# A graph and expert layer on one core: twelve gather tiles moved from the indirect DMA to SP, and reciprocal roots worked out by VectorE

## The reference

```python
# x [6250, 256]; 106250 edges (src, dst), sorted by dst; all float32
def gnn(X, src, dst, W_root, W_neigh, b):          # row = src, col = dst
    deg = segment_sum(1, row);  denom = max(deg, 1)
    neigh = segment_sum(X[col], row) / denom
    H = relu(X @ W_root + neigh @ W_neigh + b)
    gg = segment_sum((H[row] - H[col]) ** 2, row) / denom
    return tanh(gg)
def ffn(f, ...):                                   # 6 experts, the best 2 of them
    p = softmax(relu(f @ rw1 + rb1) @ rw2 + rb2)
    w = softmax(top2(p))
    return sum over the 2 of w * (relu(relu(f @ W1 + b1) @ W2 + b2) @ W3 + b3)
x = x + gnn(layernorm(x), ...)
x = x + ffn(layernorm(x), ...)                     # layernorm = (x - m) / sqrt(v + 1e-5)
```

## Time and profile before

| | |
|---|---|
| median of 3 runs | 3124.15 us (3121.96 to 3128.59) |
| the profiled execution | 3120.48 us, span 3118.7 us |
| PE | 2496.6 us busy (80%) |
| POOL | 2136.4 us busy (69%) |
| DVE | 1986.1 us busy (64%) |
| ACT | 935.7 us busy (30%) |
| mean granted clock of PE | 0.840 of full speed |
| DMA | 329.43 MB, 106 GB/s |
| edges sorted, nodes normalised | 0 to 327 us |
| first pass | 327 to 1428 us |
| H | 1428 to 1496 us |
| second pass | 1496 to 2608 us |
| first four groups, first sort | 2608 to 2678 us |
| experts, with the other groups beside them | 2678 to 3119 us |

### The profile page before, as it was taken

How to read it: one execution, slowest core, us unless ns; L and a number is a source line. 1 busy time by engine, 2 the same in 40 slices (tenths; PEclk the granted TensorE clock), 3 DMA queues, 4 the chain that set the end, 5 groups by cost and what they waited for, 6 DMA issues and landing times.

```text
span 3118.7 us, 37405 instructions
## 1 busy us (share of the span) xinstructions
PE 2496.6 (80%) x8562; PEld 1286.7 (41%) x8562; DVE 1986.1 (64%) x5179; ACT 935.7 (30%) x2562; POOL 2136.4 (69%) x2203
## 2 busy tenths in 40 slices
PE   5564688887888787889788888888888887898995
PEld 3454344343444444346322222222222222687995
DVE  8999555555554554545676767677777767566664
ACT  3689000000000000003333333333333334565653
POOL 4377677777777777778777777777777773224566
PEclk7555677777777877768999999999999998999998
DMA  0212433333333333332533333333333334344445
GB/s 29 83 4 39 136 105 106 106 105 105 106 105 105 106 105 105 106 105 92 175 105 112 105 104 104 105 105 105 105 104 105 105 105 128 100 125 130 150 146 150
DMA packets 172728, 329.43 MB, mean 106 GB/s; under 512 B 43611, under 2 KB 108833, under 8 KB 172519
## 3 DMA queue, kind: packets, MB, share of 16 engines
q0 software_dynamic: 103872, 259.13, 29.5%
q1 hardware_dynamic: 68647, 67.92, 6.6%
HBM read 284.40 MB, written 42.11 MB: 105 GB/s over the span
## 4 chain that ended last, share of the span: by engine, by line
PE 30%; POOL 26%; DMA 17%; issue 14%; DVE 10%; ACT 2%; DVEq 1%; SPq 0%; POOLq 0%; ACTq 0%
POOL arena L1047 25%; PE ps L1082 13%; DMA arena<-xn_table,graph 11%; PE ps L1905 7%; DMA arena<-h_table,graph 5%; PE ps L1879 3%; DVE big L1118 2%; DVE big L855 2%; PE ps L1208 2%; PE ps L1137 1%; DVE arena L847 1%; PE ps L1857 1%; DVE node L787 1%; PE ps L1139 1%; DVE arena L851 1%
## 5 line engine op out<-in xcount | busy, mean ns | idle before, releaser
L1082 PE MATMUL ps<-arena,graph 128*128 128x258 f32 (+1 forms) x3512 | 1714.0, 594 | 392.2 <-DMA arena<-xn_table,graph 158.9
L1118 DVE TENSOR_TENSOR big<-ps,big 128x258 f32 (+1 forms) x1756 | 982.0, 559 | 574.8 <-PE ps L1082 564.2
L1082 PEld LDWEIGHTS ps<-arena,graph 128*128 128x128 f32 x3512 | 640.1, 219 | 1450.8 <-DMA arena<-h_table,graph 747.0
L1047 POOL DMA_INDIRECT arena<-h_table,graph x878 | 840.4, 957 | 270.3 <-issue 233.2
L1047 POOL DMA_INDIRECT arena<-xn_table,graph x878 | 830.8, 946 | 282.6 <-issue 161.5
L1111 DVE TENSOR_SCALAR graph<-iota,graph 128x128 f32<-128x128 f32 x1756 | 517.5, 295 | 303.9 <-PE ps L1082 258.3
L1063 ACT ACTIVATE arena<-arena 128x256 f32<-128x256 f32 x878 | 362.6, 416 | 746.7 <-DMA arena<-h_table,graph 736.9
L1146 ACT ACTIVATE late<-ps 128x256 f32<-128x256 f32 x49 | 18.8, 383 | 924.0 <-PE ps L1127 924.0
L1485 POOL DMA_INDIRECT arena<-xn_table,node x118 | 121.5, 1030 | 240.4 <-PE ps L1857 122.9
L594 PE MATMUL ps<-big,arena 128*128 128x128 f16 x832 | 98.2, 307 | 85.2 <-ACT big L631 85.2
L541 POOL DMA_INDIRECT edge_list<-big x64 | 113.4, 1772 | 67.0 <-issue 49.4
(11 more groups left out here) (293 smaller groups left out, 1872.3 us busy)
## 6 DMA issues: line engine op xcount, KB each, us to landing
y_table<-big SPq DMA_DIRECT2D x57, 256.0 KB, 2.4
arena<-xn_table,graph POOLq DMA_INDIRECT x878, 2.7
arena<-h_table,graph POOLq DMA_INDIRECT x878, 2.7
xn_table<-node SPq DMA_DIRECT2D x7, 896.0 KB, 5.1
h_table<-node SPq DMA_DIRECT2D x7, 896.0 KB, 4.1
node<-in_x SPq DMA_DIRECT2D x1, 6144.0 KB
late<-h_table SPq DMA_DIRECT2D x12, 512.0 KB, 5.7
big<-in_x SPq DMA_DIRECT2D x12, 512.0 KB, 4.6
```

Source lines behind the costliest of these rows:

```text
L1047: e.indirect_dma_start(out=row, out_offset=None, in_=table, in_offset=bass.IndirectOffsetOnAxis(ap=idx[:, k:k + 1], axis=0)).then_inc(s_ro ...
L1082: e.matmul(out_, hot[:, k % HOTS, :], moving, start=True, stop=True).then_inc(s_sum[i], 1)
L1118: e.tensor_tensor(block, ps[a % BANKS][:, 0:width], block, ALU.add).then_inc(s_add[i], 1)
```

## The change

Six tiles of the 878 in either pass (tiles 145, 291, 437, 583, 729 and 875) are no longer gathered by POOL. SP fetches them: it loads the 128 row numbers of a tile into registers, 16 per load, and issues one DMA of 1 KB for each row. To that end DVE copies the six columns of row numbers to `sp_cols`, SP writes them to DRAM and reads two tiles' numbers at a time into one partition (`sp_row`). SP's tiles have two slots of their own, and POOL's ring has 16 slots in both passes. In the second pass SP issues five of its tiles ahead of the wait for the biases' products, and the sixth behind it.

The roots by ACT (`act_norm_root`, L1828) are gone. `dve_rsqrt` makes the reciprocal root from the variance alone: a first guess by a shift and a multiply-add on the integer form, then a step of four and a step of three operations, nine in all where it was five, each waiting for the one before. The statistics called `early` are no longer pulled ahead. In the plan route step 1 stands in the tick of step 0, and all that follows in a route moves one tick forward.

```diff
+    RING = 16
+    SPT = 6
+    LISTS = 2
@@ the first span, in dve_edges
                 if k == SUMS_AT + 2 * NA + 4:
-                    e.wait_ge(s_root, 1)
+                    e.wait_ge(s_var, 1)
                     dve_rsqrt(e, 0, NA)
@@ def act_nodes(e)
-                if b == 2 * CH - 1:
-                    act_norm_root(e, 1)
-                if b == NA + CH - 1:
-                    act_norm_root(e, 2)
@@ def dve_rsqrt(e, b0, n)
-            var, root, quot = (nsc[:, i, b0:b0 + n] for i in range(3))
-            e.reciprocal(quot, root).then_inc(s_v, 1)
...
-            e.reciprocal(rstd[:, b0:b0 + n], root).then_inc(s_v, 1)
+            var, guess, part = (nsc[:, i, b0:b0 + n] for i in range(3))
+            e.tensor_scalar(guess.bitcast(I32), var.bitcast(I32), 1, None, ALU.logical_shift_right).then_inc(s_v, 1)
+            e.wait_ge(s_v, v.up())
+            e.tensor_scalar(guess.bitcast(I32), guess.bitcast(I32), -1.0, float(0x5f3759df), ALU.mult,
+                            ALU.add).then_inc(s_v, 1)
+            for shift_by, factor in ((5.0, 1.0), (0.5625, -0.5 * 0.375 ** 3)):
+                e.wait_ge(s_v, v.up())
+                e.tensor_tensor(part, guess, guess, ALU.mult).then_inc(s_v, 1)
+                e.wait_ge(s_v, v.up())
+                e.scalar_tensor_tensor(part, part, factor, var, ALU.mult, ALU.mult).then_inc(s_v, 1)
+                if factor == 1.0:
+                    e.wait_ge(s_v, v.up())
+                    e.scalar_tensor_tensor(part, part, -10.0 / 3.0, part, ALU.add, ALU.mult).then_inc(s_v, 1)
+                e.wait_ge(s_v, v.up())
+                out_ = guess if factor == 1.0 else rstd[:, b0:b0 + n]
+                e.scalar_tensor_tensor(out_, part, shift_by, guess, ALU.add, ALU.mult).then_inc(s_v, 1)
             e.wait_ge(s_v, v.up())
@@ def dve_nodes(e)
-            dve_stats(e, a1, early)
             dve_scale(e, 1)
-            dve_stats(e, early, a2)
+            dve_stats(e, a1, a2)
...
             e.wait_ge(s_idx, 1)
+            step = NT // SPT
+            e.tensor_copy(sp_cols[:, :], idx[:, step - 1:SPT * step:step]).then_inc(s_cols, 1)
+        BY_SP = [(j + 1) * (NT // SPT) - 1 for j in range(SPT)]
+        BY_POOL_K = [k for k in range(NT) if k not in BY_SP]
+        def slot_of(k):
+
+            return RING + BY_SP.index(k) % 2 if k in BY_SP else BY_POOL_K.index(k) % RING
+
+        def sp_pass(e, i, tiles):
+
+            for j in tiles:
+                k = BY_SP[j]
+                if j >= 2:
+                    e.wait_ge(s_sum[i], BY_SP[j - 2] + 1)
+                if j % LISTS == 0:
+                    e.dma_start(sp_row, sp_list[j:j + LISTS, :].rearrange("(a j) p -> a (j p)", a=1).bitcast(I32)
+                                ).then_inc(s_sprow, 16)
+                    e.wait_ge(s_sprow, 16 * (2 + (i * SPT + j) // LISTS))
+                slot = slot_of(k)
+                row = rows2[:, slot, :] if i else rows1[:, slot, 0:D]
+                for p0 in range(0, P, 2 * OFFS):
+                    _, at_ = nc.values_load_multi_w_load_instructions(
+                        sp_row[0:1, j % LISTS * P + p0:j % LISTS * P + p0 + 2 * OFFS], engines=[mybir.EngineType.SP], min_val=0,
+                        max_val=NB * P - 1, skip_runtime_bounds_check_because="an edge's source is below N")
+                    for p, place in enumerate(at_, p0):
+                        e.dma_start(row[p:p + 1, :], (h_table if i else xn_table)[bass.ds(place, 1), :]
+                                    ).then_inc(landed(k, i)[0], 16)
+
+        def sp_first_pass(e):
+            e.wait_ge(s_cols, 1)
+            e.dma_start(sp_list.rearrange("j p -> p j"), sp_cols[:, :], allow_slow_non_contiguous=True).then_inc(s_sprow, 16)
+            e.wait_ge(s_sprow, 16)
+            e.wait_ge(s_xnout, 16 * NCH)
+            e.wait_ge(s_one, 1)
+            sp_pass(e, 0, range(SPT))
@@ def pool_pass(e, i)
-            for k in range(NT):
-                slot = k % ring
-                if k >= ring:
-                    e.wait_ge(s_sum[i], k - ring + 1)
+            for n, k in enumerate(BY_POOL_K):
+                slot = slot_of(k)
+                if n >= RING:
+                    e.wait_ge(s_sum[i], BY_POOL_K[n - RING] + 1)
@@ def route_of(pair, t)
                 put(t, "route", pair[0], 0)
-                put(t + 1, "route", pair[0], 1)
+                put(t, "route", pair[0], 1)
                 for j, g in enumerate(pair):
                     for h in half_of(g):
-                        put(t + 1 + j, "norm", g, h)
-                        put(t + 2 + j, "flip", g, h)
+                        put(t + j, "norm", g, h)
+                        put(t + 1 + j, "flip", g, h)
                     for step in (3, 4, 5):
-                        put(t + step + j, "route", g, step)
-                return t + 5 + len(pair)
+                        put(t + step - 1 + j, "route", g, step)
+                return t + 4 + len(pair)
@@ def route_slowly(pair, t)
                 put(t, "route", pair[0], 0)
-                put(t + 1, "route", pair[0], 1)
-                t += 2
+                put(t, "route", pair[0], 1)
+                t += 1
@@ def sp_records(e)
+            sp_pass(e, 1, range(SPT - 1))
             e.wait_ge(s_b3, 1 + NE)
             for g in range(1, HR):
                 sp_h_again(e, g)
+            sp_pass(e, 1, range(SPT - 1, SPT))
@@ def act_route(e, g, step)
-            if step == 0 and g in span_of:
-                b0, m = span_of[g]
-                e.wait_ge(s_ag, span_no[g] + 1)
-                e.activation(nsc[:, 1, b0:b0 + m], nsc[:, 0, b0:b0 + m], ACT.Sqrt).then_inc(s_sq2, 1)
```

More of the change, by code:

```diff
@@ L155, in gnn_moe_kernel @@
         local = graph[:, HOTS * P + NT:HOTS * P + NT + NTR]
+        sp_cols = sb("sp_cols", [P, SPT], U32)
+        sp_row = arena[0:1, SLOTS * W1 + 2 * D - LISTS * P:SLOTS * W1 + 2 * D].bitcast(I32)
+        assert SLOTS * D <= SLOTS * W1 + 2 * D - LISTS * P and (RING + 2) * W1 <= SLOTS * D
         offs = graph[0:1, HOTS * P + NT + NTR:HOTS * P + NT + NTR + P * TJ].bitcast(I32)
@@ L367, in gnn_moe_kernel @@
         s_one = sem("ones_set")
-        s_row = [sem(f"row_in_{i}") for i in range(SLOTS)]
+        s_row = [sem(f"row_in_{i}") for i in range(RING)]
+        s_rowsp = [sem(f"row_by_sp_in_{i}") for i in range(6)]
+        s_cols = sem("sp_rows_picked")
+        s_sprow = sem("sp_rows_moved")
         s_hot = [sem(f"edge_hot_made_{i}") for i in (1, 2)]
@@ L1024, in beside @@
             return k // STRIDE if k % STRIDE == 0 and k // STRIDE <= NB else None
-        def rows_in(k, i):
-            if i == 0:
-                return 16 * (k // SLOTS + 1)
-            ring = SLOTS - SQUARES
-            return 16 * (len(range(k % ring, NT, SLOTS)) + k // ring + 1)
+        BY_SP = [(j + 1) * (NT // SPT) - 1 for j in range(SPT)]
+        BY_POOL_K = [k for k in range(NT) if k not in BY_SP]
+        assert SPT % 2 == SPT % LISTS == 0 and RING + 2 + SQUARES <= SLOTS
+        def slot_of(k):
+            return RING + BY_SP.index(k) % 2 if k in BY_SP else BY_POOL_K.index(k) % RING
@@ new lines, in landed @@
+        def landed(k, i):
+            if k in BY_SP:
+                n = i * SPT + BY_SP.index(k)
+                return s_rowsp[n % len(s_rowsp)], 16 * P * (n // len(s_rowsp) + 1)
+            n, slot = BY_POOL_K.index(k), slot_of(k)
+            return s_row[slot], 16 * (i * len(range(slot, len(BY_POOL_K), RING)) + n // RING + 1)
+        def sp_pass(e, i, tiles):
[16 more added lines that the diff above has]
+                                    ).then_inc(landed(k, i)[0], 16)
@@ L1033, in pool_pass @@
+        def sp_first_pass(e):
[5 more added lines that the diff above has]
+            sp_pass(e, 0, range(SPT))
         def pool_pass(e, i):
-            table, ring = ((xn_table, SLOTS), (h_table, SLOTS - SQUARES))[i]
+            table = (xn_table, h_table)[i]
             if i == 0:
@@ L1057, in act_pass @@
                 if i:
-                    ring = SLOTS - SQUARES
-                    slot, sq = k % ring, ring + k % SQUARES
-                    e.wait_ge(s_row[slot], rows_in(k, 1))
+                    slot, sq = slot_of(k), RING + 2 + k % SQUARES
+                    e.wait_ge(*landed(k, 1))
                     if k >= SQUARES:
@@ L1318, in side_work @@
                 for j, g in enumerate(pair):
-                    put(at + 6 + j, "best", g)
+                    put(at + 5 + j, "best", g)
             x1_of(pairs[1][0], t)
@@ L1327, in side_work @@
                     y = route_slowly(pair, t)
-                    t += 2 + len(pair)
+                    t += 1 + len(pair)
                 t = y
@@ L1824, in act_route @@
             n = len(blocks)
[L1825 to L1829 removed]
+            if step == 3:
                 e.wait_ge(s_rh, g + 1)
@@ L1964, in _ @@
             sp_nodes(e)
+            sp_first_pass(e)
             sp_h(e)
```

27 lines of the change are left out of this document (6 added, 21 removed).

## The result

| | before | after |
|---|---|---|
| median | 3124.16 us (3119.66 to 3128.63, 20 runs) | 3115.27 us (3110.54 to 3122.48, 20 runs) |
| ratio | | 0.9974, 95% interval 0.9967 to 0.998 |
| profiled execution | 3120.48 us, span 3118.7 | 3113.14 us, span 3111.4 |
| granted clock | 0.840 | 0.843 |

The change makes the kernel 0.26% faster, 9 us. The forecast was 23 us, with 3113 as the upper end of its range. The direction was right, and the size was outside.

A forecast was written before the change was run, and what follows sets the result against it. POOL's gathers were taken to bound both passes, PE the expert stage. The terms +1.8 - 15.1 - 4 - 6 = -23.3 us took 3124.15 to 3101 us, range 3090 to 3113.

The forecast's parts named there:

- The bound in the passes: Both passes: each lasts as long as POOL's 878 gathers, and a gather taken off saves its period, 1.251 or 1.262 us.
- The gathers, -15.1 us: Both passes: twelve gathers leave POOL, saving 7.5 us in the first and 7.6 us in the second; smaller ring costs nothing.
- What SP pays: SP in the passes: 0.6 us per row, 77 us per tile, upper bound 0.99, hidden behind POOL's gathers.
- Rival A: Passes: SP is too slow, from 1.29 us per row, and sets their length; about 3305 us, chance 0.12.
- The fixed 2.0 us: SP's row DMAs: paid one after another, 256 us per tile against 183 allowed; the prediction went by the trace instead.
- The estimate for the DMA engines: Both passes: 16 packets per row, 24,600 more packets, 74 us of the engines' time, share 0.36 becoming 0.39.
- The start, +1.8 us: Before the first gather: DVE's four extra operations per root call delay it by 1.8 us, between 0 and 3.
- The lead stage, -4 us: Between second pass and experts: earlier variance, a table load gone and ticks saved gain 4 us, range 1.5 to 6.
- Beside the experts, -6 us: Expert stage: fewer ACT table loads shrink PE's gaps, less DVE's longer piece; 6 us won, range 0 to 11.
- four gaps of PE: Expert stage, 2680 to 2920: gaps of 1.4, 2.35, 2.49 and 3.6 us, near 10 together, laid to ACT's table loads and root waits.
- B: Whole kernel: gathers bring 15 us, roots nothing, as DVE's longer piece costs PE what ACT's tables did; 3111 us, chance 0.18.

The follow-up runs named there:

- after_again: The changed kernel, run again unaltered for a second trace: 3112.29 us, ratio 0.9972 to the kernel before.
- before_again: The kernel before, run again unaltered for a second trace: 3120.94 us, ratio 0.9995.
- list_twice: The changed kernel with SP's list of row numbers written twice, to two places, behind xn_table's writes: 3110.26 us, ratio 0.9968 to the kernel before.
- gathers_only: The kernel before plus only SP's part of the change, roots by ACT and plan as before: 3488.62 us on a chip where before takes 3485.26, ratio 1.0007.
- roots_old_plan: The kernel before with reciprocal roots by DVE as in the change; plan and gathers as before: 3125.54 us, ratio 1.0014.
- thin_old_plan: roots_old_plan with DVE's x1 and x2 pieces of groups 6 and up on 8 of 256 columns: 3108.91 us, ratio 0.9962 to the kernel before.
- thin_before: The kernel before with thin pieces: DVE works out only 8 of 256 columns of x1 and x2 for groups 6 and up: 3104.23 us, ratio 0.9939.
- thin_roots: The thin pieces of thin_before, with the change's DVE roots and plan, all gathers by POOL: 3109.9 us, ratio 0.9956 to the kernel before.
- twelve_act_roots: The kernel before plus SP fetching twelve tiles per pass, list written behind xn_table's signal, roots by ACT, plan as before: 3089.27 us, ratio 0.99.
- late_list_b: The changed kernel with SP writing the list of row numbers only once xn_table has landed: 3107.42 us, ratio 0.9951 to the kernel before.
- ring16: The kernel before with POOL's ring of 16 slots, nothing by SP: 3476.15 us on a chip where before takes 3485.26, ratio 0.9977.

## Why the prediction was wrong, step by step

**The bound in the passes** was read rightly. The passes last as long as POOL's gathers, and every gather taken off is worth its period: 12 more of them 14.6 us.

**The gathers, -15.1 us.** Right. In after_again the passes are 7.2 and 7.4 us shorter than in before_again, in list_twice 7.5 and 7.7. In the first trace of the change it is 4.6 and 5.2 against before, by its long period.

**What SP pays, 0.6 us per row (0.44 to 0.99).** It is 0.49, a tile takes 63 us, and SP is never late; the sixth tile and H's load hide as said. Rival A is dead. The smallest plain DMA plus a register's share, the lower end of my range, was the nearest row. The fixed 2.0 us of the Trainium skill ("DMA: Bandwidth & Descriptors", "Anatomy of one DMA"), which the page gives for DMAs that GpSimd issues and lays mostly to their completion, are not what SP pays to issue one: 236 rows in 116 us overlap their landings.

The estimate for the DMA engines was too high, without consequence. The hardware queue has 72,515 packets in the changed kernel against 68,647. Of the 3868 more the list takes 768 and the 1536 rows take two each, not 16, and the share in the second pass stays at 0.36.

**The start, +1.8 us.** This term failed: it was 6.4 us in the first trace of the change, and what made it up was another thing than the sum had. DVE's four extra operations are there at 0.21 us each, as worked out, but the last pieces of `xn_table` are issued no later (313.94 against 314.39). In their place stands what the sum had left out: I had counted the write of the list only as SP's own time, "starts some 8 us behind POOL", and not asked what 768 writes of 4 bytes do to the large write whose signal POOL waits for. From SP's issue of the last four pieces to the first gather it takes

| | us |
|---|---|
| 14 traces without the list behind them, or with the late list | 13.1 to 13.8 |
| after | 20.0 |
| gathers_only | 19.6 |
| list_twice | 19.2 |
| after_again | 14.4 |

The changed kernel's two rows above show it: the data of `xn_table` are under way when the list goes out at 321.94, and the list's landing (SP's next issue at 334.21) and the table's signal (POOL at 333.95) come together. So with the list queued behind it the signal comes some 6 us late in three traces of four, and 1 us late in the fourth. It is the signal and not the data that is late. In the changed kernel the 16 DMA engines move nothing from 327 to 333 us, and POOL stands (busy us of the engines, then clock, DMA share and GB/s):

```profile
327.00:333.00 6.00, 0.00 (x0) 0.00 (x0) 2.65 (x4) 0.00 (x0) 0.00 (x0) 0.50 0.00 0
```

Moved behind the signal, the list delays nothing (13.2 to 13.8 us in the five traces), and the ratio, which was 0.9968 to 0.9974, comes down to 0.9951, 5 to 7 us. Twice as many small writes do not hold it longer, so it is not a matter of their number alone; what holds it stays open.

**The lead stage, -4 us (-1.5 to -6).** Half right. On chips like the first it is 70.1 to 75.2 us in the eight traces with DVE's roots and the new plan, 72.6 in the mean, against 74.4 to 75.8 and 74.9 in the four with ACT's roots: -2.3. With DVE's roots in the plan of before it is 76.5 and 76.3 (roots_old_plan, thin_old_plan), 1.5 us above. So what is gained comes from the earlier ticks and not from the missing table loads; executions of one plan differ by up to 5 us here, so the size stays rough.

**Beside the experts, -6 us (0 to -11).** This is the step that failed most. The stage is 441.0 to 443.0 us in the seven traces with DVE's roots, the new plan and whole pieces, 441.8 in the mean, against 440.4 in the mean of three with ACT's roots: +1.3 us. The term put four gaps of PE down to ACT's table loads. roots_old_plan tests that most plainly: it has the plan of before and one table load in all. PE's seven gaps of before from 0.96 to 3.63 us (leaving out two in which it waits for its first tiles) stand there at the same matmuls, each as long as before to 0.01 us. Three of them (timeline of PE), to be held against the earlier trace rows:

```profile
2784.60 2.05 PE L1892 MATMUL ps<-arena 128*128 128x128 f32 x8 [2.35 <-issue]
...
2858.44 1.13 PE L1892 MATMUL ps<-arena 128*128 128x128 f32 x8 [2.49 <-ACT arena L1776]
...
2887.08 2.05 PE L1892 MATMUL ps<-arena 128*128 128x128 f32 x8 [3.63 <-issue]
```

Where the kernel before loads a table at 2850.10, ACT now stands idle until DVE is done:

```profile
2856.69 0.91 ACT L1746 ACTIVATE big<-big,rden 128x256 f32<-128x256 f32 x2 [1.15 <-DVE big L1543]
```

The gaps are DVE's. This is the kernel before, ahead of PE's start at 2852.99:

```profile
2848.74 1.21 DVE L1550 TENSOR_TENSOR big<-big,late 128x1024 f32<-128x1024 f32 x1
2849.98 1.23 DVE L1552 SCALAR_TENSOR_TENSOR big<-big 128x1024 f32<-128x1024 f32 x1
2851.12 1.08 DVE L1542 SCALAR_TENSOR_TENSOR big<-big,node 128x256 f32<-128x256 f32 x2
2852.20 0.70 DVE L1525 COPY arena<-node 128x1028 f32 x1
```

"x1" (L1550, L1552) stands ahead of the copy of the next tile's weights (L1525), and PE starts 0.09 us after that copy. At 2780.53 and 2880.65 it is "x2" (L1561 and L1564, 1.22 and 1.4 us) ahead of the copy, and PE starts 0.1 us after it. I took the engine that the row named for the one that was late. In the changed kernel the gap of 2.35 us is 2.36:

```profile
2768.61 1.13 PE L1942 MATMUL ps<-arena 128*128 128x128 f32 x8 [2.36 <-issue]
```

The thin pieces show the same from the other side. They leave ACT's 19 table loads in, and of nine gaps of PE of 0.9 us and more, 17.1 us together, two remain, 2.6 us:

```profile
2678.65:3103.10 424.45, 379.76 (x2847) 347.00 (x2845) 234.47 (x723) 244.65 (x704) 220.79 (x216) 0.96 0.47 143
```

DVE's roots, though, make gaps of their own. The timeline of the changed kernel's DVE and PE at the third route:

```profile
2682.60 0.63 DVE L1613 BATCH_NORM_AGGREGATE mv<-stats 128x2 f32<-128x6 f32 x8
2683.26 0.17 DVE L1615 TENSOR_SCALAR nsc<-mv 128x8 f32<-128x8 f32 x1
2683.47 0.29 DVE L945 TENSOR_SCALAR nsc<-nsc 128x8 int32<-128x8 int32 x1
...
2685.21 0.17 DVE L959 SCALAR_TENSOR_TENSOR rstd<-nsc 128x8 f32<-128x8 f32 x1
2685.41 0.17 DVE L1619 SCALAR_TENSOR_TENSOR node<-mv,rstd 128x8 f32<-128x8 f32 x1
2685.87 0.70 DVE L1566 COPY arena<-node 128x1028 f32 x1 [0.29 <-issue]
```

```profile
2684.51 0.38 PE L1894 MATMUL ps<-ident,arena 128*128 128x128 f32 x2
2686.67 1.13 PE L1942 MATMUL ps<-arena 128*128 128x128 f32 x8 [1.78 <-issue]
```

The block takes 2.98 us (2.9 was forecast), the weights' copy L1566 stands behind it, and PE waits 1.78 us, where the trace of before has no gap over 0.9 at its place. In roots_old_plan, with mean and variance a tick earlier, the rest stands behind other work of the sort, and PE still waits:

```profile
2698.98 0.74 DVE L1516 COPY arena<-node 128x1028 f32 x1 [0.30 <-issue]
```

```profile
2699.82 1.13 PE L1892 MATMUL ps<-arena 128*128 128x128 f32 x8 [1.61 <-issue]
```

Gaps of PE of 0.9 us and more beside the experts, counted from PE's timeline:

| | gaps | us together | experts |
|---|---|---|---|
| before | 9 | 17.1 | 440.5 |
| after | 13 | 21.7 | 441.1 |
| roots_old_plan | 11 | 21.3 | 444.7 |
| thin_before | 2 | 2.6 | 424.5 |
| thin_roots | 4 | 9.0 | 431.0 |
| thin_old_plan | 6 | 8.4 | 427.0 |
| twelve_act_roots | 10 | 17.8 | 440.7 |

In the other six traces of the new plan with whole pieces the gaps are 19.2 to 23.4 us. So DVE's longer roots cost PE some 3.5 us of gaps in the new plan, 4 in the old one and 6 with thin pieces, and ACT's table loads cost it next to nothing. In roots_old_plan the places can be named: right behind five of the six blocks of nine operations PE's idle time grew against before, by 1.6, 0.6, 1.0, 0.5 and 1.1 us, 4.8 us together, and the stage by 4.2. Why the new plan pays less than the old with whole pieces and more with thin ones stays open.

**The rivals.** B, "the gathers bring their 15 us and the roots nothing", at 3111 with a chance of 0.18, is what happened in outcome. Of its reasons half is right: DVE's longer piece does cost PE, but ACT's tables had cost it nothing, and what evens the roots out is the lead's gain. By the runs, 15.1 us are won by the gathers, some 6 lost to the list and 0 come from the roots, so 9 in all; the medians give 8.9. With the experts at +1.3 in place of -6 the sum would have been -16 us, 3108; with the list's 6 us as well it is 3114, against 3115.27. That the result lies only 2 us above the range is owed to B's place in it and not to foresight: the list's delay was in none of the cases.

## What to carry to other kernels

Ask of each small DMA what is in its queue ahead of it and who waits for that: a list of 3 KB in 4-byte writes delayed the start by 6 us, and one wait moved made it free. Where several engines meet at a gap, look for the one that worked through it up to its end, here DVE, take it for the cause before the engine that the row names, and be slow to move work onto it. If an engine issues without a pause and nobody is late, work taken off it pays its full period, up to what the spare engine can deliver in time: twelve tiles per pass, the list behind the signal and ACT's roots as they were give 3089 us.

## What the runs showed of the hardware

A DMA whose address comes from a register costs SP 0.49 us per row of 1 KB, with the register loads in it. 768 writes of 4 bytes need 12 to 14 us from issue to landing, about the same when sent twice (322.17 to 334.61) and when nothing is ahead of them (late_list_b, 337.01 to 349.05). In three traces of four the signal of a large write ahead of them on the queue came with theirs, 6 us late, while the 16 DMA engines stood idle or nearly so (share 0.00, 0.00 and 0.04 from 327 to 333 us). ACT's table loads of 1283 ns beside the experts were not on PE's path: without them its long gaps are the same to 0.01 us. The period of POOL's gathers can be 0.003 us longer throughout an execution, which over 1742 steps is 5 us. And a chip may run the same kernel in 3485 instead of 3124 us, with a lower granted clock (0.79 instead of 0.84), and POOL held up for PE some hundred times in a pass (ring16: 152 us in the first, 151 in the second), so that the bound of the passes is another one there; why stays open.
